# One decoder layer on one core: waits that others imply taken out, and VectorE's list put in another order

## What is computed

```
x = x + self_attn(layernorm(x))        # softmax(q k^T * scale + rel_bias) v, then @ w_out + b_out
x = x + cross_attn(layernorm(x), ctx)  # scores masked with -1e9 before the softmax, then @ Wo^T + bo
x = x + ffn(layernorm(x))

def act_quant(x):
    scale = 127 / clip(max(abs(x), axis=-1), 1e-5)
    return clip(round(x * scale), -128, 127) / scale
def ffn(y):                            # wq(w): w rounded to -1, 0, 1 times its mean absolute value
    gate = silu(act_quant(y) @ wq(w_gate).T)
    up = act_quant(y) @ wq(w_up).T
    return act_quant(gate * up) @ wq(w_down).T
```

## Time and profile before

| | before |
|---|---|
| median of 3 runs | 459.68 us |
| lowest and highest | 457.85, 462.38 us |
| span of the profiled execution, first to last instruction | 457.5 us |
| PE busy | 398.0 us (87%) |
| DVE busy | 385.7 us (84%) |
| ACT busy | 359.9 us (79%) |
| POOL busy | 329.2 us (72%) |
| mean granted TensorE clock | 0.959 of 2.4 GHz |

### The profile page before, as it was taken

How to read it: one execution, slowest core, us unless ns; L and a number is a source line. 1 busy time by engine, 2 the same in 40 slices (tenths; PEclk the granted TensorE clock), 3 DMA queues, 4 the chain that set the end, 5 groups by cost and what they waited for, 6 DMA issues and landing times. The chain is left out here.

```text
span 457.5 us, 18022 instructions
## 1 busy us (share of the span) xinstructions
PE 398.0 (87%) x5405; PEld 311.5 (68%) x5436; DVE 385.7 (84%) x1920; ACT 359.9 (79%) x962; POOL 329.2 (72%) x917
## 2 busy tenths in 40 slices
PE   3267879999999999999999999999999999877762
PEld 2245657777777777777877777778877777654430
DVE  4645467999999999999999999999999999888532
ACT  2214758899999999999999999999999998865542
POOL 6834667888888888888888888888888765654120
PEclk9998999999999999999999999999999999998655
DMA  6654577756666766676657675676567662422100
GB/s 190 162 146 100 140 188 184 173 149 172 173 159 160 191 163 168 150 195 172 170 148 196 175 175 153 164 181 170 152 158 189 165 164 80 101 78 77 30 6 13
DMA packets 100181, 67.27 MB, mean 147 GB/s; under 512 B 73269, under 2 KB 90421, under 8 KB 100085
## 3 DMA queue, kind: packets, MB, share of 16 engines
q1 hardware_dynamic: 98209, 64.08, 54.7%
q10 hardware_dynamic: 1876, 2.03, 1.5%
HBM read 46.08 MB, written 19.07 MB: 142 GB/s over the span
## 5 line engine op out<-in xcount | busy, mean ns | idle before, releaser
L895 DVE CUSTOM_DVE_ANT_0 biased<-bank,mask_bias 128x128 bf16<-128x128 f32 x512 | 112.8, 285 | 4.0 <-PE bank L1128 3.9
L900 DVE TENSOR_REDUCE neg_max_S<-bank 128x4 f32<-128x512 f32 x128 | 85.4, 675 | 21.1 <-PE bank L1128 20.4
L599 ACT ACTIVATE probs_S<-bank 128x512 f32<-128x512 f32 x128 | 72.7, 597 | 11.0 <-PE bank L1148 11.0
L599 ACT ACTIVATE probs_X<-bank 128x512 f32<-128x512 f32 x128 | 72.5, 590 | 7.0 <-PE bank L1148 6.4
L1128 PE MATMUL bank<-stack_k_S,stack_q_S 120*128 120x128 bf16 x512 | 50.5, 223 | 11.7 <-DMA stack_k_S<-scratch_S 11.0
L1148 PEld LDWEIGHTS bank<-stack_q_X,stack_k_X 74*128 74x128 bf16 x512 | 41.1, 100 | 16.6 <-issue 2.1
L1128 PEld LDWEIGHTS bank<-stack_k_S,stack_q_S 120*128 120x128 bf16 x512 | 38.6, 102 | 20.1 <-issue 11.9
L1148 PE MATMUL bank<-stack_q_X,stack_k_X 74*128 74x128 bf16 x512 | 51.4, 224 | 0.0
L1145 PE MATMUL bank<-ident_bf,mask_bias 128*128 128x512 bf16 x128 | 50.6, 396 | 0.0
L1128 PE MATMUL bank<-stack_k_X,stack_q_X 72*128 72x128 bf16 x512 | 45.3, 221 | 2.9 <-DMA stack_k_X<-scratch_X 1.7
L1166 PE MATMUL bank<-probs_X,v_aug_X 128*32 128x128 f32 x1024 | 42.4, 285 | 0.0
(11 more groups left out here) (165 smaller groups left out, 1178.6 us busy)
## 6 DMA issues: line engine op xcount, KB each, us to landing
stack_q_S<-scratch_S SPq DMA_DIRECT2D x32, 288.0 KB
stack_k_S<-scratch_S SPq DMA_DIRECT2D x32, 288.0 KB
stack_q_X<-scratch_X SPq DMA_DIRECT2D x32, 288.0 KB
stack_k_X<-scratch_X SPq DMA_DIRECT2D x32, 288.0 KB
scratch_S<-qk_parts_S SPq DMA_DIRECT2D x32, 192.0 KB, 2.7
scratch_X<-qk_parts_X SPq DMA_DIRECT2D x32, 192.0 KB, 2.7
scratch_S<-qk_parts_S SPq DMA_DIRECT2D x32, 64.0 KB, 1.7
ctxT<-ctx SPq DMA_DIRECT2D x8, 256.0 KB, 4.7
```

Source lines behind the costliest of these rows:

```text
L599: act.activation(probs[a][:, c, :], bank_b[c % 2][:, :], ACT.Exp).then_inc(sems["exp_" + a], 1)
L895: last = dve.tensor_tensor_reduce(biased[:, c, hh, :], quarter(bank_a[c % 2], hh), mask_bias[:, b % 2, :], -1.0, -2.0 * BIG, ALU.add, ALU.min,
L900: dve.tensor_reduce(neg_max[a][:, first_head(c):first_head(c) + 2 * HC - 1:2], bank_a[c % 2][:, :].rearrange("i (h j) -> i h j", h=HC), AX ...
```

## The change

Two things. First, 31 lines with a wait are taken out, on POOL, ACT, DVE and one on PE, and qk_out on ACT waits only at its first half. Each of those waits is for something that another wait, on the same engine or along the chain that leads there, already implies. No instruction is added or left out. The waits of neg_mean on mv and on xn, of h_scale on h_unit and h_q, of o_norm on oT_ps are among them.

Second, DVE's list: `h_inverse` goes from the end of a step to the beginning of the next (lag 8 becomes 9), behind residual X; out_scaling (down_scale) and ln_stats F stand ahead of h_scaling; row_max S chunk 2 stands ahead of ln_moments F, and row_max S chunk 0 ahead of ln_moments X; attend_sums X stands between gate and gated; row_max S chunk 1 stands between h_max and h_quantum. The diff, cut to its core (the removals left out are of the same kind):

```diff
@@ -408,9 +408,6 @@
                 b = st.of(k, lag)
                 if b is None or (k == "S" and b == 0 and st is not START):
                     return
-                pool.wait_ge(sems["mv_" + k], done(b))
-                if b:
-                    pool.wait_ge(sems["xn_" + k], done(b - 1))
                 pool.tensor_scalar(neg_mean[k][:], mv[k][:, 0:1], -1.0, None, ALU.mult)\
                     .then_inc(sems["neg_mean_" + k], 1)
 
@@ -624,10 +608,11 @@
                 b = st.of(a, lag)
                 if b is None:
                     return
-                act.wait_ge(sems["qkv_ps_" + a], done(b))
-                if b:
+                if m == 0:
+                    act.wait_ge(sems["qkv_ps_" + a], done(b))
+                if b and m == 0:
                     act.wait_ge(sems["rest_" + a], done(b - 1))
-                if a == "S" and b == 0:
+                if m == 0 and a == "S" and b == 0:
                     act.wait_ge(sems["dve_const"], QK_BIAS)
                 act.activation(qk[a][:, m, :], quarter(bank_p, m), ACT.Identity,
                                bias=qk_bias[a][:, m:m + 1], scale=(HD ** -0.5, 1.0)[m]).then_inc(sems[("q_", "k_")[m] + a], 1)
...
@@ -696,8 +669,6 @@
                 if b is None:
                     return
                 act.wait_ge(sems["oT_ps_" + a], done(b))
-                if b:
-                    act.wait_ge(sems["proj_" + a], done(b - 1))
                 copy(oT[a][:], quarter(bank_s, 1)).then_inc(sems["oT_" + a], 1)
 
             def tanh(st, lag):
...
@@ -790,7 +755,6 @@
                     return
                 dve.wait_ge(sems["stats_" + k], done(b))
                 if b:
-                    dve.wait_ge(sems["veps_" + k], done(b - 1))
                     dve.wait_ge(sems["neg_mean_" + k], done(b - 1))
                 dve.bn_aggr(mv[k][:], stats[k][:]).then_inc(sems["mv_" + k], 1)
 
...
@@ -915,8 +877,6 @@
                     return
                 o = bank_t[:, 0:256].rearrange("s (h e) -> s h e", h=H)
                 dve.wait_ge(sems["inv_sum_" + a], done(b))
-                if b:
-                    dve.wait_ge(sems["oT_ps_" + a], done(b - 1))
                 dve.tensor_tensor(o_norm[a][:], o[:, :, 0:HD],
                                   inv_sum[a][:].unsqueeze(2).to_broadcast([S, H, HD]), ALU.mult)\
                                       .then_inc(sems["o_norm_" + a], 1)
...
@@ -1013,9 +966,6 @@
                 if b is None:
                     return
                 dve.wait_ge(sems["h_inv"], done(b))
-                dve.wait_ge(sems["h_unit"], done(b))
-                if b:
-                    dve.wait_ge(sems["h_q"], done(b - 1))
                 dve.tensor_tensor(h_scale[:], h_inv[:], h_unit[:], ALU.mult).then_inc(sems["h_scale"], 1)
 
             def residual_ffn(st, lag):
...
@@ -1028,12 +978,13 @@
                                          ALU.mult, ALU.add).then_inc(sems["res_F"], 1)
 
             def step(st):
+                residual("X", st, 8)
+                h_inverse(st, 9)
+                out_scaling(st, 9)
+                ln_stats("F", st, 8)
                 h_scaling(st, 9)
-                residual("X", st, 8)
-                ln_stats("F", st, 8)
-                out_scaling(st, 9)
+                row_max("S", st, 3, 2)
                 ln_moments("F", st, 8)
-                row_max("S", st, 3, 2)
                 row_max("S", st, 3, 3)
                 row_max("X", st, 6, 0)
                 residual_ffn(st, 9)
@@ -1054,16 +1005,15 @@
                 mean_weights(st, -1)
                 ternary_weights(st, -1)
                 ln_stats("X", st, 4)
+                row_max("S", st, 2, 0)
                 ln_moments("X", st, 4)
-                row_max("S", st, 2, 0)
                 gate(st, 8)
+                attend_sums("X", st, 7)
                 gated(st, 8)
-                attend_sums("X", st, 7)
                 attend_norm("X", st, 7)
                 h_max(st, 8)
+                row_max("S", st, 2, 1)
                 h_quantum(st, 8)
-                h_inverse(st, 8)
-                row_max("S", st, 2, 1)
 
             run(step)
 
@@ -1158,7 +1108,6 @@
                 if c == 0:
                     if a == "S" and b == 0:
                         pe.wait_ge(sems["dve_const"], QK_BIAS)
-                    pe.wait_ge(sems["v_" + a], done(b))
                     after(pe, st, *users)
```

38 lines of the change are left out of this document (removed).

## The result

| | kernel before | changed kernel |
|---|---|---|
| time, median of 6 runs each | 459.37 us (457.85 to 462.38) | 486.74 us (484.82 to 488.80) |
| ratio | | 1.057, 95% interval 1.054 to 1.061 |
| span of the profiled execution | 457.5 us | 483.0 us |
| instructions in the trace | 18022 | 16633 |
| start of the first y_max | 82.01 | 83.40 |

The changed kernel is 27 us slower; the two medians by themselves give a ratio of 1.060, inside the interval. The span grew by 25.5 us: 18.2 of it in the 26 steps (0.70 each), 5.9 behind them, 1.4 ahead of them.

The account below looks back on a forecast made before the run. Two nearly equal loops of waits into y_max, through xn_F and through residual_ffn, were taken as the bound. Span 457.5 + 14.3 (26 steps) + 5.5 (tail) = 477.3 us, median about 479.5, range 467 to 488 us.

Parts of the forecast that it names:

- The two loops: Paths to y_max, via mv_F and xn_F, and via h_scale, h_q, down matmuls and residual_ffn; both arriving within 0.05 us.
- Step (1): Waits taken out: nothing on VectorE; on GpSimd neg_mean_F starts earlier, saving 0.12 us a step, or nothing.
- Step (2): Dependent VectorE neighbours parted: six gaps of 0.12 us plus some 0.06 at mv_F, 0.77 us a step saved.
- Rival D: Gaps stay though neighbours are parted, each operation waiting for the one in front: near 499 us, chance 0.02.
- Step (3): inv_sum_X ahead of h on VectorE: held 0.67 us for TensorE's transposes, delaying the operations behind it.
- Rival A: Faster: inv_sum_X finds its transposes done, held under 0.25 us; median near 453 us, chance 0.07.
- Step (4): Residual X ahead of h_inv and h_scale on VectorE: waits for proj_X, behind o_norm_X, adding 0.18 us.
- Rival B: Milder loss: inv_sum_X held, proj_X in time, tail hides half; step 0.30 us longer, near 470.5 us, chance 0.16.
- Step (5): row_max S chunk 2 ahead of mv_F on VectorE: 0.59 us of queue; mv_F ends 0.82 us later in all.
- From y_max to h_gate: VectorE's stretch before h_gate: mv_X's gap of 0.12 us goes, of which 0.10 us a step is kept.
- The sum: Step longer by 0.60 us, taken as 0.55; 26 steps give 14.3 us, the span 477.3 us, the median about 479.5.
- The tail: Five more steps where the h_scale loop binds and residual X now precedes h_scale: 1.1 us each, 5.5 us.

Follow-up runs that it names:

- e4: Changed kernel with mv_F put back ahead of row_max S chunk 2: 484.61 us, 1.052 of the kernel before.
- e5: Changed kernel with h_inv, down_scale and h_scale put back ahead of residual X: 482.56 us, 1.047 of the kernel before.
- e45: Changed kernel with mv_F back ahead of row_max S chunk 2 and h_inv, down_scale, h_scale back ahead of residual X: 474.19 us, 1.030.
- e3: Changed kernel with h put back between h_gate and inv_sum_X, covering the transposes: 484.34 us, 1.053 of the kernel before.
- e8: Changed kernel with mv_X put back ahead of row_max S chunk 0: 480.92 us, 1.041 of the kernel before.
- e1: Changed kernel with VectorE's list as in the kernel before, implied waits still out: 460.17 us, 0.997 of the kernel before.
- e2: Changed kernel with its new order but all waits of the kernel before put back: 487.23 us, 1.056 of the kernel before.
- e6_inv_alone: Kernel before with one exchange, inv_sum_X ahead of h: 470.47 us, 1.021 of the kernel before.

## Why the prediction was right, and where a step was off

**The bound.** The two loops named in the forecast are the bound, and the sentence that mending one alone would not help is what e4, e5 and e45 show: 0.03, 0.05 and 0.32. The 0.05 us within which they were to arrive is right by luck: it was worked out for y_max behind residual_ffn, where there is 0.25 us of room (GpSimd's gap stayed, 0.12, and from the end of h_scale to residual_ffn it is 2.55 us and not 2.65), and the loops meet at inv_sum_S, with 0.04. One of the signs named did not come: residual_ffn was to be idle a few tenths in each step, and it is idle for 1.2 us in 26, 0.05 each. The forecast that the loss would sit in the 26 steps and in the part behind them holds as well: 18.2 against 14.3 us, and 5.9 against 5.5.

**Step (1), the waits.** Right on VectorE, wrong on GpSimd. neg_mean_F was to follow veps_F directly and to save 0.12 us a step; it kept its 0.08 us of gap, and GpSimd's part is 2.35 us as before. The gap is not the wait's. The lower bound stated for this term, nothing, is what came. This is 3.1 us in 26 steps, most of the 3.9 by which the sum over the steps fell short.

**Step (2), the parted neighbours.** The gaps at h, o_norm_X, h_step, h_inv and stats_F went from 0.03 after the end to 0.08 before it. (h_inv was at 243.62 behind a forerunner that ended at 243.59; it is at 255.13 beside one that ends at 255.21.) Their worth came, and some 0.13 us more, because the records of h_gate, h and the other parted operations are shorter too (below). mv_X's gap did not go: row_max S c0, which now stands behind stats_X (250.07 to 250.36), starts at 250.40, 0.03 after it, since TensorE's scores for it end at 250.37. So the gap was handed on to c0. (The 3.9 us of idle in the row of row_max S, 0.5 before, are this only for 0.9 us; 3.0 us stand ahead of chunk 3, behind mv_F.) Rival D is out: no parted operation had to wait until the one in front of it was through. The sentence on the DRAIN in the Trainium skill's page VectorE: DVE Perf Modes, weighed in the forecast, does not describe the parted operations in these rows, which start 0.08 us before the end of the one in front. No run takes the partings alone, so what they are worth is read from rows and not from a time.

**Step (3), the hold of inv_sum_X.** Forecast 0.67, measured 0.59 of idle and 0.08 of overlap, in every one of the 26 steps; 19.1 us in all, inside the 16 to 21 that were named. Rival A hung on this hold being under 0.25. But e3 adds what the forecast did not say: in the changed kernel this hold alone moves nothing, because proj_X would be late without it.

**Step (4), residual X.** Forecast 0.18, measured 0.27 and 0.08 of overlap, 0.35. The size is off by 0.17, and the reason given was the wrong one. It was put down to o_norm_X; e8 shows it to be mv_X, which the forecast booked only as a gap saved. The failing step is that the move of mv_X was not followed beyond VectorE: mv_X behind a row_max, veps_X on GpSimd late (17.0 us of waiting against 3.0), xn_X late, TensorE idle for 0.40 us in the middle of its list, proj_X late. Rival B had proj_X in time; e8 comes nearest to it, at 480.9 us, not 470.5, and its tail of 77.4 us was not milder.

**Step (5), row_max ahead of mv_F.** 255.52 to 256.12 is 0.60 of the queue, forecast 0.59. All together mv_F ends 0.86 us later behind h_gate, forecast 0.82: residual X was 0.17 more, shorter records 0.13 less. The sum is good because two errors of opposite sign met.

**From y_max to h_gate.** It shrank by 0.16 us, forecast 0.10, but not by mv_X's gap: inv_sum_S, which had 1.5 us of idle and 0.08 of lost overlap each time, has 0.3 and starts without waiting.

**The sum.** A step is 0.70 longer in place of 0.55: 0.12 from the GpSimd gap that stayed, 0.04 from mv_F, 0.05 from the allowance that the row_max and transposes would shift with TensorE, which they did not, less 0.06 from the stretch to h_gate. With 1.4 us ahead of the steps, which may be nothing, and 0.4 behind them this is the 5.7 us between the forecast's span and the measured one. The median is 7.2 us above the forecast's 479.5 and 1.3 us below the upper end of its range, 488: the other 1.5 us is that the profiled execution was the fastest of the six, 3.7 us of span below the median, where the forecast took 2.2.

**The tail.** Forecast 5.5, measured 5.9, and the mechanism, residual X ahead of h_scale where the second loop is the bound, is shown by e5, which takes 4.3 of it back. e3, which takes the hold of inv_sum_X away, has a tail of 71.7 us, 2.8 shorter; the two parts are not independent, since they come to more than the loss. Each tail is that of one profile: with the list as before they are 68.6 and 67.6 us (kernel before, e1), with the new list 74.5 and 75.7 (changed kernel, e2).

## What to carry to other kernels

Before parting two dependent neighbours for 0.1 us, write beside each moved instruction who waits for its result on every other engine, and follow that to the end: here mv_X, mv_F and h_scale each feed another engine; mv_X and mv_F went behind a 0.6 us row_max each and h_scale behind residual X, and with the hold of inv_sum_X this cost more than all the gaps together were worth. An operation that stands idle is not thereby the one that costs time (taken out of the changed kernel alone, the 15.4 us of inv_sum_X gave 0.02 us a step), and where two or three paths close within a few hundredths of a microsecond an edit has to shorten all of them: measure the pair, not only its parts. Waits that others already imply cost nothing that could be measured here.

## What was not expected of the hardware

- The records of several VectorE operations are shorter when their producer is not right in front of them: h takes 687 ns directly behind h_gate (kernel before, and again in e3_h_covers) and 628 behind inv_sum_X (changed kernel, e6_inv_alone); mv_X 182 behind stats_X (kernel before, and again in e8_mvX_first) and 172 behind a row_max; h_inv 164 and 153, o_norm_X 291 and 277. So a parted pair gains 0.115 and a further 0.01, and h 0.06. Whether it is the dependence or the instruction in front that counts is open: mv_F took 182 ns with one small operation between it and stats_F (down_scale in the kernel before, h_scale in e4_mvF_first) and 172 with a row_max between them as well; and h_gate went from 678 to 653 ns when mv_X in place of a row_max stood ahead of it (back to 678 in e8_mvX_first), and it depends on neither.
- On GpSimd neg_mean_F starts 0.08 us after the end of veps_F with a wait on it or without, while rstd_F behind it starts 0.03 us before the end of neg_mean_F. No run here shows what makes it so.
